# A macaron block on one Trainium2 core: four more turned experts, and a planner with new margins

## The chip, the cores and the metric

The program runs on one core of one Trainium2 chip. A core has TensorE (PE, matrix products into the eight banks of PSUM), VectorE (DVE), ScalarE (ACT), GpSimd (POOL) and SyncE (SP), which issues transfers. Each engine takes its own instructions in order and waits at semaphores for the others. The metric is the time of one execution in microseconds.

## The reference

The block works on 4 sequences of 1024 rows with 128 features in fp32:

```
x = x + 0.5 * ffn(layernorm(x))        # first mixture of experts
x = x + mamba(layernorm(x))            # selective state space layer
x = x + 0.5 * ffn(layernorm(x))        # second one, the same weights

ffn:   cw = softmax(x @ w_router) * softmax(x @ w_gating / 0.1), normalised   # 8 weights per row
       out = sum over e of cw[:, e] * ((silu(x @ w_gate[e]) * (x @ w_up[e])) @ w_down[e])
mamba: h_t = exp(dt_t * A) * h_{t-1} + dt_t * B_t * u_t;  y_t = C_t . h_t     # 256 channels, 16 states
```

All eight experts are computed for every row: F = 512 hidden columns, 128 features.

## The kernel before

**Tiles and positions.** The rows are cut into 8 tiles of 512. Each tile goes once through the first mixture, kind 0, once through the state space layer, and once through the second mixture, kind 1. The 16 passes through a mixture are the positions of ORDER: position 0 is (0, 0), tile 0 first mixture; position 15 is (1, 7).

**Slots.** A position has 32 slots, one for each of 8 experts times 4 chunks of 128 hidden columns; slots are counted through, so position 14 is slots 448 to 479 and position 15 is 480 to 511. In a slot PE makes the gate product (step `first_g`, three products of 512 columns, L839, L840, L842, with high and low parts of the operands), the up product (step `first`, the same three lines) and the down product (step `down`). ACT makes silu of the gate (L1306), DVE multiplies it with up to h (HB, L1113). The gate runs two slots ahead (AHEAD), the down product two slots behind (LAG): in PE's order stand first_g(i+2), first(i), down(i-2).

**Ordinary and turned experts.** In an ordinary expert the down product has h as its stationary operand and is made in fp32, four products of 128 columns (L920); the result lies with rows on partitions. In a turned expert (TURNS) the weights are stationary, the result is transposed, and the down product is three products of 512 columns: high weights with high h (L910), low weights with high h (L912), high weights with low h (L914). For this h is rounded into HI (step `h_hi`) and the remainder made as HL by DVE (`h_lo`, L1069), and the weights of two chunks at a time are split into WDS (`wd_hi`, a rounding, and `wd_lo`, L1081 on DVE). Before the change ACT makes all roundings. WDS has two buffers, HI three.

**Weighing.** The result of an expert is multiplied by its column of weights (step `acc`: L1331 on ACT, L1106 on DVE, L1050 for turned ones) into YE, and added to the tile XT by a transfer that GpSimd issues (L1439). For turned experts the weights must be rows: CW is transposed by PE (`cw_t`, L930), stored to CWD in DRAM and loaded broadcast into YE (`cw_load`, L811); the sum goes into AT, is turned back by four transposes (`t_tr`, L940) and added to XT (`t_add`).

**State space steps.** Each tile has 16 scans (one for each state) of two halves on DVE (`s_b` L1200, `s_scan` L1211, `s_hc` L1219), which need rows of B and C broadcast into BCB by SyncE (`bc_load`, L799, three buffers), and whose results GpSimd's transfers add into Y. `s_yz` closes a tile on DVE (L1231, L1233; for the last tile two additions stand before the product), `s_out` is the output product on PE (L969). The products before the scans are `b_in`, `b_x` and `b_dt`; `b_conv` is the convolution on DVE (L1164). The router of a position is `p_logits` on PE, then `p_max` (L1015 to L1021), `p_exp` on ACT, and `p_norm`, `p_sum`, `p_cw` (L1026 to L1040) on DVE.

**What sets the order.** `timetable()` plays the kernel once with estimated costs, keeping a clock for each engine (`clock`), and writes one list of steps. Each engine's program is that list with the steps that are its own. So a number in the planner moves instructions, and a wait on the chip holds up all that stands behind it on that engine. The planner does not wait for `h_lo` or `wd_lo` when it places `down`. `x_load` brings a later tile into the buffer (XR = 5) of an earlier one and waits in SyncE's queue until the store of that one has landed.

## Time and profile before

| | us |
|---|---|
| median of 3 runs | 1252.88 (1252.73 to 1253.44) |
| the profiled execution | 1252.7 |
| span of its profile | 1250.9 |
| PE busy | 1244.1 (99%) |
| DVE busy | 1131.1 (90%) |
| ACT busy | 1017.1 (81%) |
| POOL busy | 388.4 (31%) |

The span is the time from the first to the last instruction of the program; the execution is 1.8 us longer. PE is on the chain that ended last for 96% of the span. Rows of PE and DVE overlap each other on the same engine, since these engines are pipelined, so the cost of an instruction among others is read from start to start. The granted clock of TensorE is 1.00 in the whole profile, its upper level of 2.4 GHz.

### The profile page before, as it was taken

How to read it: one execution, taken by the hardware profiler on the slowest of the kernel's cores; microseconds unless marked ns; L12 is line 12 of the kernel's file. 1: busy time of each engine (PE TensorE's matmuls, PEld its weight loads, DVE VectorE, ACT ScalarE, POOL GpSimd, SP SyncE). 2: the span in 40 equal slices, each digit the busy share in tenths (PEclk: the TensorE clock that was granted, in tenths of full speed). 3: DMA queues.
4: the chain of work that ended last, by engine and by line, in shares of the span. 5: the costliest groups of instructions: out<-in, count | busy, mean ns of one | idle time of the engine just before them, and what ended most of it. 6: DMA issues, size and time to landing. Idle time of an engine off the chain costs nothing.

```text
span 1250.9 us, 20830 instructions
## 1 busy us (share of the span) xinstructions
PE 1244.1 (99%) x7311; PEld 1076.0 (86%) x7311; DVE 1131.1 (90%) x1524; ACT 1017.1 (81%) x2079; POOL 388.4 (31%) x455
## 2 busy tenths in 40 slices
PE   9999999999999999999999999999999999999998
PEld 6887888888888888888888888888888888888887
DVE  5857699999999999999999999999999989998476
ACT  6777988888987887989978899798987979765664
POOL 0010134234333333334234333352434433332100
PEclk9999999999999999999999999999999999999999
DMA  7412368797878787878898798987979887895132
GB/s 225 105 24 42 87 132 172 144 196 161 168 143 178 161 174 151 177 153 172 164 201 160 153 194 172 186 172 151 199 148 190 154 160 158 161 191 112 28 75 51
DMA packets 116809, 185.90 MB, mean 149 GB/s; under 512 B 11264, under 2 KB 31840, under 8 KB 116704
## 3 DMA queue, kind: packets, MB, share of 16 engines
q0 software_dynamic: 55760, 101.74, 46.1%
q1 hardware_dynamic: 60944, 82.83, 26.4%
q8 instruction: 57, 0.93, 0.3%
q14 instruction: 48, 0.39, 0.1%
HBM read 80.15 MB, written 2.67 MB: 66 GB/s over the span
## 4 chain that ended last, share of the span: by engine, by line
PE 96%; ACT 2%; DVE 1%; issue 1%; DMA 0%; POOL 0%; DVEq 0%; ACTq 0%
PE PS L920 32%; PE PS L839 19%; PE PS L842 19%; PE PS L840 19%; PE PS L969 1%; PE PS L954 1%; PE PS L912 1%; PE PS L914 1%; PE PS L910 1%; PE PS L861 1%; PE PS L871 1%; ACT DA L1401 0%; PE PS L961 0%; ACT HB L1306 0%; DVE HL L1069 0%
## 5 line engine op out<-in xcount | busy, mean ns | idle before, releaser
L920 PEld LDWEIGHTS PS<-WD,HB 128*128 128x128 f32 x3616 | 472.2, 191 | 37.6 <-issue 0.5
L920 PE MATMUL PS<-WD,HB 128*128 128x128 f32 x3616 | 476.0, 274 | 0.0
L1113 DVE TENSOR_TENSOR HB<-PS,HB 128x512 f32<-128x512 f32 x512 | 348.3, 681 | 85.7 <-PE PS L842 72.8
L1306 ACT ACTIVATE HB<-PS 128x512 f32<-128x512 f32 x512 | 294.6, 597 | 111.2 <-PE PS L842 108.7
L1456 POOL DMA_DIRECT2D Y<-HS x252 | 222.1, 958 | 369.2 <-DVE HS L1219 186.4
L839 PE MATMUL PS<-XH,WG 128*128 128x512 f32 x512 | 238.7, 466 | 0.8 <-DVE WG L1120 0.6
L1439 POOL DMA_DIRECT2D XT<-YE x111 | 105.4, 949 | 318.9 <-ACT YE L1331 166.8
L839 PE MATMUL PS<-XH,WU 128*128 128x512 f32 x512 | 203.7, 398 | 0.0
L842 PE MATMUL PS<-XH,WG 128*128 128x512 f32 x512 | 202.2, 395 | 0.0
L842 PE MATMUL PS<-XH,WU 128*128 128x512 f32 x512 | 201.6, 394 | 0.0
L840 PE MATMUL PS<-XH,WG 128*128 128x512 f32 x512 | 200.3, 391 | 0.0
L840 PE MATMUL PS<-XH,WU 128*128 128x512 f32 x512 | 200.3, 391 | 0.0
L1401 ACT ACTIVATE DA<-XS,aneg 128x512 f32<-128x512 f32 x256 | 164.3, 713 | 0.8
L1211 DVE TENSOR_TENSOR_SCAN HS<-DA,car,HS 128x512 f32<-128x512 f32 x128 | 161.8, 1275 | 0.0
L1219 DVE TENSOR_TENSOR HS<-BCB,HS 128x1024 f32<-128x1024 f32 x128 | 156.1, 1220 | 1.4
L1200 DVE TENSOR_TENSOR HS<-BCB,DX 128x1026 f32<-128x1026 f32 (+1 forms) x128 | 155.5, 1220 | 0.2
L1211 DVE TENSOR_TENSOR_SCAN HS<-DA,HS 128x513 f32<-128x513 f32 x128 | 153.8, 1217 | 0.1
L840 PEld LDWEIGHTS PS<-XH,WU 128*128 128x128 f32 x512 | 96.5, 188 | 22.6 <-issue 0.5
L842 PEld LDWEIGHTS PS<-XH,WU 128*128 128x128 f32 x512 | 96.0, 187 | 22.8
L839 PEld LDWEIGHTS PS<-XH,WU 128*128 128x128 f32 x512 | 96.1, 188 | 22.7 <-issue 0.5
L842 PEld LDWEIGHTS PS<-XH,WG 128*128 128x128 f32 x512 | 96.1, 188 | 22.6 <-DVE XH L1171 0.4
L1306 ACT ACT_TABLE_LOAD x87 | 111.6, 1283 | 2.1 <-PE PS L842 0.6
(133 smaller groups left out, 1343.7 us busy)
## 6 DMA issues: line engine op xcount, KB each, us to landing
BCB<-BCD SPq DMA_DIRECT2D x128, 512.0 KB, 5.3
Y<-HS POOLq DMA_DIRECT2D x252, 256.0 KB, 6.3
XT<-YE POOLq DMA_DIRECT2D x111, 256.0 KB, 4.9
YE<-CWD SPq DMA_DIRECT2D x15, 256.0 KB, 4.7
XS<-DX POOLq DMA_DIRECT2D x7, 512.0 KB, 9.0
AT<-YE POOLq DMA_DIRECT2D x11, 256.0 KB, 3.3
XT<-in_L_attn_x_dram SPq DMA_DIRECT2D x8, 256.0 KB, 6.6
WD<-in_L_ffn_w_down_dram SPq DMA_DIRECT2D x8, 256.0 KB, 6.4
```

Source lines behind the costliest of these rows:

```text
L839: pe.matmul(o, w[0], m[0], start=True, stop=False)
L840: pe.matmul(o, w[1], m[0], start=False, stop=False)
L842: pe.matmul(o, w[0], m[1], start=False, stop=True).then_inc(S[sem], 1)
L920: z = pe.matmul(part(g, j), HB[:, i % NH, j * P:(j + 1) * P], WD[:, e, c, :], start=c == 0 and j in firsts, stop=c == FC - 1 and j in lasts)
L1113: v.tensor_tensor(H, up(i), H, ALU.mult).then_inc(S["v_h"], 1)
L1200: v.tensor_tensor(HS[:, m % HR, :, 0:w], rows.unsqueeze(1).broadcast_to([P, 2, w]), DX[:, t % 2, :, 0:w], ALU.mult).then_inc(S["v_db"], 1)
L1211: v.tensor_tensor_scan(H, DA[:, m % NA, j, 0:w], H, car[:, j, n:n + 1] if t % 2 else 0.0, ALU.mult, ALU.add).then_inc(S["v_sc"], 1)
L1219: v.tensor_tensor(H, BCB[:, m % BR, 1, :].unsqueeze(1).broadcast_to([P, 2, T]), H, ALU.mult).then_inc(S["v_hc"], 1)
L1306: a.activation(HB[:, i % NH, :], gate(i), ACT.Silu).then_inc(S["a_sil"], 1)
L1401: z = a.activation(DA[:, m % NA, j, 0:T], XS[:, t % 2, j, 3:3 + T], ACT.Exp, scale=aneg[:, j, n:n + 1])
L1439: gp.dma_start(to, buffer(g), accum_op=ALU.add).then_inc(S["c_acc"], 16)
L1456: gp.dma_start(Y[:, t % 2, j, :], HS[:, m % HR, j, 0:T], accum_op=ALU.add).then_inc(S[f"c_y{j}"], 16)
```

## The change

Experts 4 to 7 of position 14 become turned, so that turned slots run from 464 through 507. Which engine rounds h and the weights is no longer a matter of the position: the planner gives a rounding to ACT where ACT's clock is early, else to DVE. The weights of a pair are split one slot sooner (SPLIT = 2 instead of 1). Turned results other than a run's last are weighed two or three down products later. The passes (1, 3) and (0, 7) change places. The load of a later x tile may be issued from slot 2 of the position before, as soon as the planner has placed the store of the tile whose buffer it takes. Margins of the planner change with it.

```diff
-ORDER = [(0, 0), (0, 1), (0, 2), (0, 3), (1, 0), (0, 4), (1, 1), (0, 5), (1, 2), (0, 6), (1, 3), (0, 7), (1, 4), (1, 5), (1, 6), (1, 7)]
+ORDER = [(0, 0), (0, 1), (0, 2), (0, 3), (1, 0), (0, 4), (1, 1), (0, 5), (1, 2), (0, 6), (0, 7), (1, 3), (1, 4), (1, 5), (1, 6), (1, 7)]
...
-CALM = 0.9
-LATEST = 0.2
+CALM = 0.8
+LATEST = 0.3
...
-TURNS = {0: range(2, 6), 1: range(1, 5), 15: range(0, 7)}
-SCALAR_PARTS = (0, 1, 15)
+TURNS = {0: range(2, 6), 1: range(1, 5), 14: range(4, 8), 15: range(0, 7)}
+EASY = 0.4
+SPLIT = 2
...
+TURN_LATER = 2
+WEIGHED_LATER = {g: BEGIN_LATER if g in TURN_BEGINS else TURN_LATER for g in TURNED if g not in TURN_ENDS}
...
+        if what[0] == "x":
+            yield from until(loaded_x.get(what[1], 0.0))
...
-            at = step("b_add", t, after=at, p=.9) + 7.0
+            at = step("b_add", t, after=at, p=.9) + SUMMED
...
-        scanned[t] = y_at[1]
+        scanned[t] = y_at[1] + SETTLED
...
-        if "scans" in streams and (haste or turn[0] % (3 if passed[0] < NS // 2 else 1) == 0):
+        if HURRY and "scans" not in streams and not begun["scans"]:
+            advance("before")
+        elif "scans" in streams and (haste or turn[0] % (3 if passed[0] < NS // 2 else 1) == 0):
...
     def high(i):
-        on = {"a": .53} if i // SLOTS in SCALAR_PARTS else {"v": .35}
-        hi_at[i] = step("h_hi", i, after=h_at[i], **on)
+        if clock["a"] < h_at[i] + EASY:
+            scalar_rounds.add(i)
+            hi_at[i] = step("h_hi", i, after=h_at[i], a=.53)
+            low(i - 1)
+        else:
+            low(i - 1)
+            hi_at[i] = step("h_hi", i, after=h_at[i], v=.35)
...
+    def split(i):
+        if clock["a"] < clock["pe"] + EASY:
+            scalar_splits.add(i)
+            at = step("wd_hi", i, a=.31)
+        else:
+            at = step("wd_hi", i, v=.2)
+        return at
...
-            if nd % FC == BEGIN_LATER and nd // FC - 1 in TURN_BEGINS:
+            if nd // FC - 1 in WEIGHED_LATER and nd % FC == WEIGHED_LATER[nd // FC - 1]:
...
                 weigh(nd // FC - 1)
-            if (nd + 1) % PAIR == 0 and nd + 1 in TURNED_SLOTS:
...
+            m = nd + SPLIT
+            if m % PAIR == 0 and m in TURNED_SLOTS:
+                split_at[m] = split(m)
+                if m not in scalar_splits:
+                    step("wd_lo", m, v=.4)
...
-        if r == LOADR and p + 1 < NPOS and ORDER[p + 1][0] == 0 and ORDER[p + 1][1] >= XR:
-            step("x_load", ORDER[p + 1][1])
+        if r >= LOADR and p + 1 < NPOS and ORDER[p + 1][0] == 0:
+            t = ORDER[p + 1][1]
+            if t >= XR and t not in asked_x and t - XR in stored_out:
+                asked_x.add(t)
+                loaded_x[t] = max(clock["pe"], stored_out[t - XR] + STORED) + LOADED
+                step("x_load", t)
```

Counted in the built programs, 36 roundings of weights stand on DVE instead of none and 2 on ACT instead of 30; of h, 7 on DVE and 69 on ACT instead of 60 on ACT. There are 76 turned slots instead of 60.

The lines of the changed kernel are numbered 37 higher behind the planner: L1113 is L1150 there, L1069 L1106, L1081 L1118, L1231 L1268, L1233 L1270, L1015 L1052, L1026 L1063, L1040 L1077, L799 L836, L823 L860, L816 L853.

DVE at the closing of the last tile (the first turned slot of position 14, 464; Y<-Y,HS and Y<-Y,SZ are the closing, HB<-PS,HB the product h of a slot, HL and WDS the low parts of h and of the weights). Before:

```order
L1219 TENSOR_TENSOR HS<-BCB,HS 128x2x512
L1113 TENSOR_TENSOR HB<-PS,HB 128x512
L1231 TENSOR_TENSOR Y<-Y,HS 128x1024 x2
L1233 TENSOR_TENSOR Y<-Y,SZ 128x1024
L1113 TENSOR_TENSOR HB<-PS,HB 128x512 x3
```

and now:

```order
L1256 TENSOR_TENSOR HS<-BCB,HS 128x2x512
L1150 TENSOR_TENSOR HB<-PS,HB 128x512 x2
L1268 TENSOR_TENSOR Y<-Y,HS 128x1024 x2
L1270 TENSOR_TENSOR Y<-Y,SZ 128x1024
L1118 TENSOR_TENSOR WDS<-WD,WDS 128x256
L1150 TENSOR_TENSOR HB<-PS,HB 128x512
L1106 TENSOR_TENSOR HL<-HB,HI 128x512
```

The second of the two HB<-PS,HB is h of slot 464; its low part, the last row, stands behind the closing.

DVE at the second half of position 15's router (lg to CW are its softmax and weights), which stands at the end of position 14, slots 478 to 480. Before:

```order
L1113 TENSOR_TENSOR HB<-PS,HB 128x512
L1026 TENSOR_TENSOR lg<-lg 128x4x8
L1028 TENSOR_REDUCE zz<-lg 128x12
L1031 SCALAR_TENSOR_TENSOR sm<-zz 128x4
L1034 TENSOR_TENSOR sm<-sm,zz 128x4
L1038 RECIPROCAL sm<-sm 128x4
L1040 SCALAR_TENSOR_TENSOR CW<-lg,sm 128x32
L1113 TENSOR_TENSOR HB<-PS,HB 128x512 x3
```

and now:

```order
L1102 CAST HI<-HB 128x512
L1063 TENSOR_TENSOR lg<-lg 128x4x8
L1065 TENSOR_REDUCE zz<-lg 128x12
L1068 SCALAR_TENSOR_TENSOR sm<-zz 128x4
L1071 TENSOR_TENSOR sm<-sm,zz 128x4
L1075 RECIPROCAL sm<-sm 128x4
L1077 SCALAR_TENSOR_TENSOR CW<-lg,sm 128x32
L1087 TENSOR_TENSOR YE<-PS,YE 128x512
L1113 CAST WDS<-WD 128x256
L1118 TENSOR_TENSOR WDS<-WD,WDS 128x256
L1150 TENSOR_TENSOR HB<-PS,HB 128x512
L1106 TENSOR_TENSOR HL<-HB,HI 128x512
```

The router's chain has a weighing, a split of weights and two roundings of h for neighbours, and HL of slot 479 is the last row.

SyncE around the store of tile 2 (out_dram) and the load of x tile 7 (XT<-in). Before:

```order
L823 DMA out_dram<-XT 128x4x128
L799 DMA BCB<-BCD 128x2x512 x8
L816 DMA XT<-in_L_attn_x_dram 128x4x128
L799 DMA BCB<-BCD 128x2x512 x9
L792 DMA BCD<-XN 32x512
```

and now:

```order
L836 DMA BCB<-BCD 128x2x512 x11
L860 DMA out_dram<-XT 128x4x128
L853 DMA XT<-in_L_attn_x_dram 128x4x128
L829 DMA BCD<-XN 32x512
L836 DMA BCB<-BCD 128x2x512 x17
```

The load stood eight BCB loads behind the store, and now stands directly behind it.

## Rows read from the trace of the kernel before

**Rows 1.** Windows: span, busy us (x instructions) PE PEld DVE ACT POOL, PEclk, DMA, GB/s.

```profile
160.00:1160.00 1000.00, 999.30 (x6083) 875.76 (x6082) 962.77 (x1205) 841.42 (x1701) 363.49 (x419) 1.00 0.83 166
1141.00:1181.00 40.00, 40.00 (x251) 35.40 (x250) 23.94 (x37) 21.78 (x59) 4.93 (x7) 1.00 0.22 38
```

**Rows 2.** Timeline of PE, ordinary slot: start us, us, engine line op.

```profile
281.76 0.48 PE L839 MATMUL PS<-XH,WG 128*128 128x512 f32 x1
282.08 0.40 PE L840 MATMUL PS<-XH,WG 128*128 128x512 f32 x1
...
284.05 0.48 PE L839 MATMUL PS<-XH,WG 128*128 128x512 f32 x1
```

**Rows 3.** Timeline of PE, a turned slot of position 15.

```profile
1207.28 0.39 PE L839 MATMUL PS<-XH,WG 128*128 128x512 f32 x1
...
1209.34 0.39 PE L839 MATMUL PS<-XH,WG 128*128 128x512 f32 x1
```

**Rows 4.** Timeline of PE, transposes at 1183 and 1244 us.

```profile
1183.40 0.27 PE L930 MATMUL PS<-CON,CW 128*32 128x128 f32 x1
...
1244.46 0.60 PE L940 MATMUL PS<-CON,AT 128*128 128x128 f32 x4
1244.89 2.29 PE L920 MATMUL PS<-WD,HB 128*128 128x128 f32 x19
```

**Rows 5.** Timeline of PE, position 1: waits for WDS, first, third and last.

```profile
102.24 0.50 PE L912 MATMUL PS<-HI,WDS 128*128 128x512 f32 x1
...
117.55 0.39 PE L910 MATMUL PS<-HI,WDS 128*128 128x512 f32 x1
118.20 0.50 PE L912 MATMUL PS<-HI,WDS 128*128 128x512 f32 x1 [0.27 <-DVE WDS L1081]
118.55 0.39 PE L914 MATMUL PS<-HL,WDS 128*128 128x512 f32 x1
...
128.78 0.50 PE L912 MATMUL PS<-HI,WDS 128*128 128x512 f32 x1 [0.32 <-DVE WDS L1081]
```

**Rows 6.** Timeline of DVE among turned slots of position 1.

```profile
117.72 0.42 DVE L1081 TENSOR_TENSOR WDS<-WD,WDS 128x256 fp32r<-128x256 f32 x1
118.06 0.69 DVE L1050 TENSOR_TENSOR YE<-PS,YE 128x512 f32<-128x512 f32 x1
118.66 0.69 DVE L1113 TENSOR_TENSOR HB<-PS,HB 128x512 f32<-128x512 f32 x1
```

**Rows 7.** Timeline of DVE, the product h behind PE at 1183 us.

```profile
1183.67 0.69 DVE L1113 TENSOR_TENSOR HB<-PS,HB 128x512 f32<-128x512 f32 x1 [1.59 <-PE PS L842]
```

**Rows 8.** Groups by line and shape: xcount | busy us, mean ns | idle.

```profile
L1133 DVE CAST WI<-DA 128x512 fp32r<-128x512 f32 x1 | 0.4, 422 | 0.0
...
L1164 DVE SCALAR_TENSOR_TENSOR Y<-XS,cw_t,Y 128x512 f32<-128x512 f32 x48 | 34.6, 745 | 0.0
```

**Rows 9.** Timeline of DVE, the closing of the last tile.

```profile
1149.67 2.55 DVE L1231 TENSOR_TENSOR Y<-Y,HS 128x1024 f32<-128x1024 f32 x2
...
1153.40 1.28 DVE L1113 TENSOR_TENSOR HB<-PS,HB 128x512 f32<-128x512 f32 x2
```

**Rows 10.** Timeline of DVE, router of position 15.

```profile
1173.34 0.31 DVE L1015 STREAM_TRANSPOSE LT<-LR 128x128 f32<-128x128 f32 x1 [0.83 <-ACT LR L1294]
...
1174.55 0.69 DVE L1113 TENSOR_TENSOR HB<-PS,HB 128x512 f32<-128x512 f32 x1
...
1177.43 0.18 DVE L1026 TENSOR_TENSOR lg<-lg 128x32 f32<-128x32 f32 x1
...
1178.55 0.19 DVE L1040 SCALAR_TENSOR_TENSOR CW<-lg,sm 128x32 f32<-128x32 f32 x1
```

**Rows 11.** SyncE: the stores' landing (L823), then its queue's timeline.

```profile
DMA to landing us min/median/max: 2.3/5.7/10.5
...
731.62 0.47 SPq L823 DMA_DIRECT2D out_dram<-XT  x1
737.14 7.20 SPq L799 DMA_DIRECT2D BCB<-BCD  x2
```

More of the change, by code:

```diff
@@ L441, in timetable, with low @@
     nd = 0
-    hi_at = {}
+    hi_at, split_at = {}, {}
     def high(i):
-        on = {"a": .53} if i // SLOTS in SCALAR_PARTS else {"v": .35}
-        hi_at[i] = step("h_hi", i, after=h_at[i], **on)
+        if clock["a"] < h_at[i] + EASY:
[5 more added lines that the diff above has]
+            hi_at[i] = step("h_hi", i, after=h_at[i], v=.35)
+    def low(i):
+        if i in hi_at:
+            step("h_lo", i, after=hi_at[i], v=.6)
+    def split(i):
[5 more added lines that the diff above has]
+        return at
     for i in range(total):
@@ L456, in timetable @@
         h_at[i] = clock["v"] + SIGNAL["v"]
-        if i in TURNED_SLOTS and p in SCALAR_PARTS:
+        if i in TURNED_SLOTS:
             high(i)
-        if i - 1 in hi_at:
-            step("h_lo", i - 1, after=hi_at[i - 1], v=.6)
-        if i in TURNED_SLOTS and p not in SCALAR_PARTS:
-            high(i)
+        else:
+            low(i - 1)
         side()
@@ L466, in timetable @@
             nd += 1
-            if nd % FC == BEGIN_LATER and nd // FC - 1 in TURN_BEGINS:
+            if nd // FC - 1 in WEIGHED_LATER and nd % FC == WEIGHED_LATER[nd // FC - 1]:
+                if nd % SLOTS // FC == 1:
+                    finish("prep")
                 weigh(nd // FC - 1)
-            if (nd + 1) % PAIR == 0 and nd + 1 in TURNED_SLOTS:
-                on = {"a": .31} if (nd + 1) // SLOTS in SCALAR_PARTS else {"v": .2}
-                step("wd_hi", nd + 1, **on)
-                if "v" in on:
-                    step("wd_lo", nd + 1, v=.4)
-            if nd % PAIR == 0 and nd in TURNED_SLOTS and nd // SLOTS in SCALAR_PARTS:
-                step("wd_lo", nd, v=.33)
+            m = nd + SPLIT
[3 more added lines that the diff above has]
+                    step("wd_lo", m, v=.4)
+            m -= 1
+            if m in scalar_splits:
+                step("wd_lo", m, after=split_at[m], v=.35)
             row_loads()
@@ L479, in timetable @@
             elif nd % FC == 0:
-                if nd % SLOTS == FC:
+                if nd % SLOTS == FC and nd // FC - 1 not in TURNED:
                     finish("prep")
-                if nd // FC - 1 not in TURN_BEGINS:
+                if nd // FC - 1 not in WEIGHED_LATER:
                     weigh(nd // FC - 1)
@@ L494, in timetable @@
                 step("small_load")
-            if r % 2 and 25 <= r <= 29:
-                step("set", (r - 25) // 2, v=1.4)
-        if r == LOADR and p + 1 < NPOS and ORDER[p + 1][0] == 0 and ORDER[p + 1][1] >= XR:
-            step("x_load", ORDER[p + 1][1])
+        if i in SETS:
+            step("set", SETS.index(i), v=1.4)
+        if r >= LOADR and p + 1 < NPOS and ORDER[p + 1][0] == 0:
[4 more added lines that the diff above has]
+                step("x_load", t)
         if p + 1 < NPOS and r >= (PREP if p != 1 else LATER) and p + 1 not in prepared:
@@ L514, in timetable @@
     run(tail(NPOS - 1))
-    return steps, scalar_weighs
+    return steps, scalar_weighs, scalar_rounds, scalar_splits
 class Waits:
@@ L533, in macaron_program @@
     of = out.rearrange("b (t j p) d -> (b t) p j d", t=2, j=SUB)
-    steps, scalar_weighs = timetable()
+    steps, scalar_weighs, scalar_rounds, scalar_splits = timetable()
     with ExitStack() as ctx:
@@ L663, in rows_loads @@
             return f"c_cw{BUFFERED.index(g) % 2}", 16 * len(same)
-        def scalar_part(i):
-            return i // SLOTS in SCALAR_PARTS
         def wait_high(eng, i):
-            sem = "a_hh" if scalar_part(i) else "v_hh"
-            eng.wait_ge(S[sem], sum(k <= i and scalar_part(k) == scalar_part(i) for k in TURNED_SLOTS))
+            by_scalar = i in scalar_rounds
+            same = [k for k in TURNED_SLOTS if k <= i and (k in scalar_rounds) == by_scalar]
+            eng.wait_ge(S["a_hh" if by_scalar else "v_hh"], len(same))
         def wait_weights_high(eng, i):
-            sem = "a_wd" if scalar_part(i) else "v_wh"
-            eng.wait_ge(S[sem], sum(k <= i and scalar_part(k) == scalar_part(i) for k in TURNED_SLOTS if k % PAIR == 0))
+            by_scalar = i in scalar_splits
+            same = [k for k in TURNED_SLOTS if k <= i and k % PAIR == 0 and (k in scalar_splits) == by_scalar]
+            eng.wait_ge(S["a_wd" if by_scalar else "v_wh"], len(same))
         def pair(i):
@@ L1060, in _ @@
                     v.tensor_tensor(X, X, bank(b), ALU.add).then_inc(S["v_at"], 1)
-                elif k == "h_hi" and not scalar_part(s[1]):
+                elif k == "h_hi" and s[1] not in scalar_rounds:
                     i = s[1]
@@ L1070, in _ @@
                                     ).then_inc(S["v_hl"], 1)
-                elif k == "wd_hi" and not scalar_part(s[1]):
+                elif k == "wd_hi" and s[1] not in scalar_splits:
                     i = s[1]
@@ L1312, in _ @@
                     a.activation(LR[0:SUB * E, :], bank(b)[0:SUB * E, 0:P], ACT.Copy).then_inc(S["a_ct"], 1)
-                elif k == "h_hi" and scalar_part(s[1]):
+                elif k == "h_hi" and s[1] in scalar_rounds:
                     i = s[1]
@@ L1317, in _ @@
                     a.activation(HI[:, TURNED_SLOTS[i] % HI_RING, :], HB[:, i % NH, :], ACT.Copy).then_inc(S["a_hh"], 1)
[L1318 removed]
+                elif k == "wd_hi" and s[1] in scalar_splits:
                     i = s[1]
```

19 lines of the change are left out of this document (14 added, 5 removed).

## The prediction

> **What bounds the kernel now.** I read the windows first. In the thousand microseconds in which the state space stages run, TensorE (PE) is busy 999.3 us and VectorE (DVE) 962.8 us [rows 1], so the time is PE's list of products plus whatever PE waits, and the waits are small. What has to be counted is products removed, products added, and waits lost or gained. In the stretch where the four experts are turned (about 1141 to 1181 us) DVE was busy 23.9 us of 40 [rows 1], which looks like ample room for the new work. A mean over 40 us says nothing about single places, though, and DVE takes its instructions strictly in order, so I then followed DVE's order through the new slots, with the timeline of DVE and PE for the spacing.
>
> **The change part by part.**
>
> *Removed: one product per turned slot.* An ordinary slot is six products of 512 columns and four fp32 ones that the trace shows as eight. From one L839 to the same point a slot later it takes 284.05 - 281.76 = 2.29 us, in which L839 to L840 is 0.32 us instead of the 0.23 us that such a product needs elsewhere, a loss of 0.09 us behind fp32 products [rows 2]. A turned slot is nine products of 512 columns: 1209.34 - 1207.28 = 2.06 us [rows 3], with no such loss. Saved per slot 0.23 us; 16 slots: -3.7 us, all on PE, which is the bound.
>
> *Added on PE.* Position 14 gets its own transposes: four of AT, 1244.89 - 1244.46 = 0.43 us, plus 0.09 us for the product behind them, since they now stand among 512 column products; and one of the weights, which at 0.43/4 comes to 0.11 us [rows 4]. The output product of the last tile (s_out, fp32) now also stands among 512 column products: 0.09 us. Together +0.7 us. Net on PE: -3.0 us.
>
> *Waits that go: weights split a slot sooner.* In position 1, PE waits in four slots between L910 and L912 for the low part of the weights (WDS from L1081). The first ends at 102.24, the last at 128.78; in the third L910 to L912 takes 118.20 - 117.55 = 0.65 us where an undisturbed step is 0.23, and the product behind it is late as well, 0.35 instead of 0.23 us [rows 5]. Read in the same way the four exceed the undisturbed step by 0.25, 0.11, 0.42 and 0.49 us, and with some 0.1 us each behind them that is 1.7 us. With the split issued one slot sooner DVE has a slot (2.06 us) more than it needs, so all four go: -1.7 us. What is late next is the low part of h (HL, read by L914).
>
> *Waits that come.* For each new or changed place I add up DVE's instructions from the product h of a slot to its own HL, and compare with what PE does from the end of that slot's up product to L914. Prices are start to start, since a row's duration overlaps the next: a full width operation 118.66 - 118.06 = 0.60 us, the low split of a weight pair 118.06 - 117.72 = 0.34 us [rows 6]. h starts 0.27 us after PE's next product, L930 at 1183.40 against 1183.67 [rows 4, 7], and 0.05 us more pass before PE starts: WDS ends at 117.72 + 0.42 = 118.14, L912 starts at 118.20 [rows 5, 6]. A cast of 512 columns lasts 0.42 us, taken as 0.35 start to start, one of 256 as 0.20 [rows 8].
>
> Place A, slot 464, the first turned one. The closing of the last tile (two adds, one product) stands between h(464) and the split. It costs 1153.40 - 1149.67 = 3.73 us [rows 9], since each waits for the one before. DVE: h 0.60 + 3.73 + WDS 0.34 + h(465) 0.60 + HL 0.68 to its end + 0.32 = 6.27 us. PE gets there after two ordinary slots and two products: 4.58 + 0.46 = 5.04 us. PE waits 1.2 us, with the late product behind it 1.3 us. Before, no turned slot was here, and the closing cost PE nothing.
>
> Place B, slots 477 to 479. The router of position 15 now stands among turned slots. DVE: four h 2.40, three HL 1.80, the last to its end 0.68, the maximum chain 1174.55 - 1173.34 = 1.21, the softmax chain L1026 to L1040 1178.55 - 1177.43 and the start of the next, 1.23 [rows 10], two weight pairs 1.08, two casts of h on DVE 0.70, one weighing 0.60, latency 0.32: 10.02 us. PE: four turned slots and two products, 8.24 + 0.46 = 8.70 us. PE waits 1.3 us, 1.4 with the product behind.
>
> Place C, slots 44 to 47, position 1: five h 3.00, four HL 2.40 and 0.68, six convolution steps at 0.66 (0.75 us each [rows 8], less the same 0.09 of overlap), a copy 0.07, two weighings 1.20, two weight pairs 1.08, latency 0.32: 12.71 us. PE: five turned slots, six products of b_in and two more, 10.30 + 1.38 + 0.46 = 12.14 us. 0.6 us, with what is late behind 0.7 us.
>
> These three cost +3.4 us. They are bounds from below where DVE comes late to the place, from above where PE has been held up for other reasons between; both unknowns I put at 0.5 us each way.
>
> Here a rule of the Trainium skill is weighed, VectorE: DVE Perf Modes, section The DRAIN you can't avoid: an instruction does not start until the pipe of the one before has emptied. The row shows 0.60 us from start to start of instructions of 0.69 us [rows 6], so here the next one starts before the row's end, and the measurement decides. What it would make of the time stands with the rivals.
>
> *Edits costed at nothing.* Rounding by timetable moves 28 weight casts from ScalarE to DVE and some castings of h; their DVE time is in A, B and C, and elsewhere in the turned stretches a pair of slots has 4.11 us for at most 4 h or HL (2.40) + 0.54 + a weighing 0.60 = 3.54 us. If that cover were gone, each pair would cost the difference. Weighing two products later: the expert's bank is read again a slot group later (8.2 us), so 4.1 us more are free; only B's weighing lies on a bad place, and it is counted. The new AT and YE transfers go through GpSimd's and SyncE's queues after the last scan transfer, where nothing of DVE waits for them. The swap of (1,3) and (0,7) and the new margins of the planner re-order the middle. There PE was idle 0.7 us of 1000 [rows 1]; overlapping rows hide short waits, so the gain is at most some 2 us, and a loss as large is as likely. I take 0.
>
> *The x tile.* In the new order the load of tile 7 stands directly behind the store of tile 2 in SyncE's queue and waits until that store has landed; behind it stand a row store (BCD) and the loads of BCB that DVE needs. The next such load followed the store by 737.14 - 731.62 = 5.5 us before, and stores land in 2.3 to 10.5 us, median 5.7 [rows 11]. At the median plus two issues of 0.4 us the BCB load is 1.0 us late, and I take that as hidden by the three buffers of BCB; at 10.5 us it is 5.8 us late. Bounds 0 and +5.8 us; I take 0, the row of the median being nearest.
>
> **Sum.** -3.7 + 0.7 - 1.7 + 3.4 = -1.3 us. On the profiled execution, 1252.7 us with a span of 1250.9 us, that is 1251.4 us; on the median of the runs, 1252.88 us, it is **1251.6 us**. A measurement of this kernel can tell about 0.2%, 2.5 us, from no change, so my forecast lies within it.
>
> **Rivals.**
>
> *The waits A and B do not appear* (the planner's order gives DVE enough lead, or PE is late there for other reasons). Then -3.7 + 0.7 - 1.7 + 0.7 = -4.0 us: 1248.9 us. For it: DVE was busy 60% in that stretch [rows 1]. Against it: h cannot start before its product, so DVE's lead does not help; the sums start there. With only one of the two: 1250.3 us. Chance 0.21 in all.
>
> *The store holds SyncE's queue.* The load of x waits for the store at 10.5 us, BCB is 5.8 us late, and DVE, 96% busy there [rows 1], stands still with the products h behind that row's first operation; PE's product two slots on waits for h. It decides from a store landing of about 6 us. At worst -1.3 + 5.8 = +4.5 us, 1257.4 us; at 8 us 3.3 us late: 1254.9 us. This is the case on the slower side. For it: stores that long exist. Against it: the buffers. Chance 0.12, of which 0.07 over 2.5 us slower.
>
> *DVE's instructions do not overlap in the new mixture.* Each then costs its whole row: 0.69 us for h, HL and a weighing, 0.42 for WDS and a wide cast, 0.75 for a convolution step [rows 6 to 8]. A comes to 1.5 us, B to 2.4, C to 2.5, with the products behind 6.7 instead of 3.4 us: +2.0 us, 1254.9 us. Against it: the very instructions of the turned slots stand 0.60 us apart [rows 6]. Chance 0.03. This is what the page named above would give.
>
> *The split is not sooner in effect.* If the casts wait for the bank (each waits for the product that frees its buffer), PE still waits at L912: the 1.7 us stay, 1253.3 us. Chance 0.08. The Trainium skill, SBUF — State Buffer, section Who interferes with whom, says that an fp32 copy from SBUF to SBUF on DVE holds GpSimd off, descriptors included, and that the second to come waits wholly. By that rule each of the 43 new casts could hold a transfer's issue for its own length, or be held by it. No row of this case shows it.
>
> **How the numbers follow.** Forecast, between 1250.4 and 1253.2 us: 0.56. Waits absent 0.21, queue 0.12, splits 0.08, no overlap 0.03. The range takes in one of A and B missing together with a gain in the middle (1249.4) and the queue's case at 8 us (1254.9): 1249.4 to 1254.9. Faster by over 0.2% (under 1250.4): the first rival, 0.21, with 0.01 from the middle. Slower by over 0.2%: 0.07 of the queue. Within: 0.71.
>
> **What the new profile would show.** Right: sixteen more slots of 2.06 us; PE waiting about 1.2 us for HL, between the second and the third product of a turned slot, around 1148 us and again around 1181 us, with no wait for WDS in position 1 but one for HL; SyncE's load of x issued 5 to 8 us behind the store. Wrong: turned slots of position 14 without a wait (the sums' start is wrong), waits for WDS again (buffers, not order), or DVE waiting for BCB near 740 us. A new PE wait of more than 2 us in the middle would break the zero that I took there.

## The result, and the profile after

The changed kernel takes 1256.13 us (median of 10 runs, 1254.23 to 1257.52), the kernel before in the same session 1252.91 us (10 runs, 1252.20 to 1254.15): a ratio of 1.0026, 95% interval 1.0017 to 1.0034. It is slower by about 3.2 us, and the forecast of 1251.6 us, with its range of 1249.4 to 1254.9 us, was wrong. The profiled execution took 1255.67 us with a span of 1253.9 us, against 1252.7 and 1250.9 us.

All line numbers are 37 higher than before. The windows answer to [rows 1]; the third shows where the time went. Columns: span, busy us (x instructions) of PE, PEld, DVE, ACT, POOL, PEclk, DMA share, GB/s.

```profile
160.00:1160.00 1000.00, 998.75 (x6061) 874.54 (x6060) 969.60 (x1221) 843.42 (x1693) 368.74 (x417) 1.00 0.81 166
...
1141.00:1181.00 40.00, 39.07 (x189) 31.63 (x189) 34.79 (x66) 25.28 (x59) 3.72 (x5) 1.00 0.19 42
...
130.00:160.00 30.00, 28.11 (x163) 24.14 (x162) 21.28 (x31) 27.57 (x60) 5.16 (x8) 1.00 0.35 91
```

The middle is as busy as before. Where position 14's experts are turned, DVE went from 23.9 to 34.8 us of 40 and PE stood still for 0.9 us. Between 130 and 160 us, a stretch that the prediction did not look at, PE stood still for 1.9 us. The waits of PE name it (line, releaser, us in total, times, longest):

```profile
PE PS L951 <- DVE HL L1106: 2.0, 3, 1.1
PE PS L977 <- DMA AT<-YE: 1.9, 1, 1.9
...
PE PS L977 <- DVE AT L1092: 1.2, 1, 1.2
```

The first line holds the waits that were forecast. The other two, 3.1 us, were not: L977 are the transposes with which a group of turned experts ends, in position 1 and at the end of the kernel. None of the rows of before shows PE waiting there.

I also went through all products of both traces, 7311 before and 7236 after, from start to start, and took from each the median step of its kind in the kernel before, as the undisturbed one (0.23 us for 512 columns, 0.32 behind fp32, 0.11 for fp32 of 128 columns). The undisturbed steps come to 1238.1 us before and 1235.4 us after, so the product saving is there, 2.7 us. What lies above them went from 7.9 to 13.6 us. The prices below called an excess are from this reckoning; an excess is that of the wait alone, and the product behind a wait for HL or WDS is late by another 0.10 to 0.11 us each time.

**The forecast waits.** PE at places A, B and C, and a turned slot (answering [rows 3]):

```profile
1147.43 0.40 PE L947 MATMUL PS<-HI,WDS 128*128 128x512 f32 x1
1147.94 0.50 PE L949 MATMUL PS<-HI,WDS 128*128 128x512 f32 x1
1149.14 0.50 PE L951 MATMUL PS<-HL,WDS 128*128 128x512 f32 x1 [0.70 <-DVE HL L1106]
...
1183.14 0.39 PE L949 MATMUL PS<-HI,WDS 128*128 128x512 f32 x1
1184.67 0.50 PE L951 MATMUL PS<-HL,WDS 128*128 128x512 f32 x1 [1.14 <-DVE HL L1106]
...
118.00 0.50 PE L951 MATMUL PS<-HL,WDS 128*128 128x512 f32 x1
...
120.53 0.50 PE L951 MATMUL PS<-HL,WDS 128*128 128x512 f32 x1 [0.18 <-DVE HL L1106]
...
1207.03 0.39 PE L876 MATMUL PS<-XH,WU 128*128 128x512 f32 x1
...
1209.11 0.39 PE L876 MATMUL PS<-XH,WU 128*128 128x512 f32 x1
```

Excess at A 0.28 + 0.97 = 1.25 us, at B 1.30 us, at C 0.13 + 0.34 = 0.47 us. The forecast counted the products behind as well; with them it is A 1.35 us (forecast 1.3), B 1.41 us (1.4) and C 0.86 us (0.7), where a third, shorter wait follows at 124.8 us. A turned slot takes 2.08 us (2.06). DVE at place A, where the closing stands ahead of the low part of the weights and of h:

```profile
1143.14 0.69 DVE L1150 TENSOR_TENSOR HB<-PS,HB 128x512 f32<-128x512 f32 x1 [0.82 <-PE PS L879]
1143.74 2.55 DVE L1268 TENSOR_TENSOR Y<-Y,HS 128x1024 f32<-128x1024 f32 x2
1146.33 1.23 DVE L1270 TENSOR_TENSOR Y<-Y,SZ 128x1024 f32<-128x1024 f32 x1
1147.47 0.42 DVE L1118 TENSOR_TENSOR WDS<-WD,WDS 128x256 fp32r<-128x256 f32 x1
1147.81 0.68 DVE L1150 TENSOR_TENSOR HB<-PS,HB 128x512 f32<-128x512 f32 x1
1148.41 0.68 DVE L1106 TENSOR_TENSOR HL<-HB,HI 128x512 fp32r<-128x512 f32 x1
```

HL ends at 1149.09, and PE's L951 starts at 1149.14. The step from h to HL is 0.60 us, as in [rows 6].

**The waits nobody forecast.** AT collects what the turned experts of a position produce, by transfers that add YE into it, issued by GpSimd (POOL) one after the other: each waits until the one before has landed. These are the three of position 1, before and then after (start us, us from issue, what POOL waited for):

```profile
119.05 0.86 POOL L1439 DMA_DIRECT2D AT<-YE  x1 [20.45 <-DVE YE L1050]
129.62 0.85 POOL L1439 DMA_DIRECT2D AT<-YE  x1 [9.71 <-DVE YE L1050]
138.49 0.86 POOL L1439 DMA_DIRECT2D AT<-YE  x1 [8.02 <-DMA AT<-YE]
```

```profile
123.24 0.86 POOL L1476 DMA_DIRECT2D AT<-YE  x1 [24.05 <-DVE YE L1087]
132.84 0.85 POOL L1476 DMA_DIRECT2D AT<-YE  x1 [8.74 <-DVE YE L1087]
141.69 0.86 POOL L1476 DMA_DIRECT2D AT<-YE  x1 [7.99 <-DMA AT<-YE]
```

The second one lands 8.3 us after its issue in both, the third 3.25 us after. In both kernels the third waits for the second, so the end of the chain moves with the weighing of expert 3, which DVE now does at 131.86 instead of 128.64 us. The third lands at 138.49 + 3.25 = 141.74 us before, at 141.69 + 3.25 = 144.94 us after. PE's transposes, first before the change and then after it:

```profile
143.34 0.60 PE L940 MATMUL PS<-CON,AT 128*128 128x128 f32 x4
```


```profile
142.12 1.05 PE L957 MATMUL PS<-WD,HB 128*128 128x128 f32 x8
145.07 0.63 PE L977 MATMUL PS<-CON,AT 128*128 128x128 f32 x4 [1.89 <-DMA AT<-YE]
```

An excess of 2.06 us. Before, AT was there 1.6 us ahead of PE; it now comes 3.2 us later, and PE is ready for it 0.3 us earlier. At the end of the kernel the last transfer into AT has DVE as its next link (POOL, then DVE, then PE); the transfer before it had landed at 1236.4 us and holds nothing up:

```profile
1242.25 0.86 POOL L1476 DMA_DIRECT2D AT<-YE  x1 [8.34 <-issue]
```

```profile
1240.39 0.68 DVE L1087 TENSOR_TENSOR YE<-PS,YE 128x512 f32<-128x512 f32 x1
...
1246.60 0.69 DVE L1092 TENSOR_TENSOR AT<-AT,YE 128x512 f32<-128x512 f32 x1 [1.94 <-DMA AT<-YE]
```

```profile
1247.44 0.63 PE L977 MATMUL PS<-CON,AT 128*128 128x128 f32 x4 [1.22 <-DVE AT L1092]
```

Before, that weighing stood at 1235.11 and its transfer at 1236.09 us. Excess 1.39 us. Three things add up here: the weighing is two products later, the transfer is issued 1.86 us behind the start of its weighing instead of 0.98, and it lands 4.26 us after its issue instead of 3.30. The first is the edit; what the other two come from, no run shows.

**The clock behind the wait.** In 7 of the 10 runs the mean granted clock of TensorE was 0.999 (1255.98 to 1257.52 us), in the other three 1.0 (1254.23, 1255.17, 1255.67 us), medians 1256.41 and 1255.17 us; in the kernel before it was 1.0 in all. The profiled execution of after shows nothing of it; that of e7, which has the same wait, does (PE, then the window and, below it, the same stretch of the changed kernel's own profile):

```profile
144.81 0.63 PE L977 MATMUL PS<-CON,AT 128*128 128x128 f32 x4 [1.94 <-DMA AT<-YE]
145.19 0.61 PE L876 MATMUL PS<-XH,WG 128*128 128x512 f32 x1
145.61 0.63 PE L877 MATMUL PS<-XH,WG 128*128 128x512 f32 x1
146.03 0.63 PE L879 MATMUL PS<-XH,WG 128*128 128x512 f32 x1
```

```profile
144.80:148.20 3.40, 3.39 (x13) 2.81 (x14) 2.69 (x3) 2.42 (x5) 0.00 (x0) 0.59 0.02 5
```

```profile
144.80:148.20 3.40, 3.13 (x20) 2.85 (x21) 2.43 (x3) 2.99 (x6) 0.00 (x0) 1.00 0.02 5
```

Behind the wait the granted clock is at its lower level, 1.2 instead of 2.4 GHz (0.59 on the mean of this window), and a step takes 0.42 us instead of 0.23. Six such steps are 1.2 us.

### The profile page after: what moved, and what is told of

Its sections match the earlier page's. It is cut to its first block, busy times and chain, and to the rows that moved or that the text cites. A ratio compares the mean times of both kernels' runs of the same rounds, so it can differ in the third digit from the quotient of the medians.

```text
span 1253.9 us, 20727 instructions
## 1 busy us (share of the span) xinstructions
PE 1242.1 (99%) x7236; PEld 1071.0 (85%) x7236; DVE 1159.2 (92%) x1598; ACT 1011.0 (81%) x2037; POOL 395.0 (32%) x454
## 4 chain that ended last, share of the span: by engine, by line
PE 92%; DVE 2%; DMA 2%; ACT 2%; issue 1%; SPq 0%; DVEq 0%; POOLq 0%; ACTq 0%
PE PS L957 30%; PE PS L876 18%; PE PS L879 18%; PE PS L877 18%; DMA AT<-YE 2%; PE PS L1006 1%; PE PS L951 1%; PE PS L991 1%; PE PS L947 1%; PE PS L949 1%; PE PS L898 1%; PE PS L908 1%; DVE HB L1150 1%; DVE HL L1106 1%; ACT L1343 0%
## 5 line engine op out<-in xcount | busy, mean ns | idle before, releaser
L957 PEld LDWEIGHTS PS<-WD,HB 128*128 128x128 f32 x3488 | 455.7, 191 | 36.6 <-issue 0.5
L957 PE MATMUL PS<-WD,HB 128*128 128x128 f32 x3488 | 459.2, 274 | 0.0
L1150 DVE TENSOR_TENSOR HB<-PS,HB 128x512 f32<-128x512 f32 x512 | 347.8, 680 | 62.8 <-PE PS L879 46.8
```

Source lines behind the costliest of these rows:

```text
L957: z = pe.matmul(part(g, j), HB[:, i % NH, j * P:(j + 1) * P], WD[:, e, c, :], start=c == 0 and j in firsts, stop=c == FC - 1 and j in lasts)
L1150: v.tensor_tensor(H, up(i), H, ALU.mult).then_inc(S["v_h"], 1)
```

## The experiments

Theory: the loss is the late weighing, by the chain of transfers into AT, at two places, with the lower clock behind the first; the product saving and the waits A, B and C are as forecast. Rivals: the turned experts of position 14 cost more than they save; the splits or the new order do. Every time below is a median of 11 runs unless said otherwise, beside the kernel before in the same session: 1252.74 us for e1 to e4, 1252.76 for e5 to e8, 1253.11 for e9 to e12.

### The late weighing taken back, in whole and by place

e1: every weighing at once, but for the first expert of a group, which was late before the change too.

```diff
-WEIGHED_LATER = {g: ... for g in TURNED if g not in TURN_ENDS}
+WEIGHED_LATER = {g: ... for g in TURN_BEGINS}
```

> The changed kernel with the turned results weighed as before the change: right after the last down product of their expert, the first of a run one product earlier; the rest of the change stays. Theory (the later weighing makes the two turns back late: PE waits 2.06 us for the transfer into AT before position 1's transposes, 1.39 us for the last sum at the end, and the weighing lies in the router's place at slot 479): both waits go, and the wait at slot 479 shrinks from 1.3 to about 0.7 us, so 4.0 us less than the changed kernel, about 1252.1 us, and the transfers into AT are issued 3 to 4 us earlier. Rival (the casts on DVE hold GpSimd off, or its queue is late for another reason): the waits for AT stay above 1 us each and the time stays above 1254.5 us.

Measured 1252.77 us, ratio 1.0000 (0.9990 to 1.0009). Both waits for AT are gone and the clock is 1.0 in all runs. The casts are all still on DVE, so the rival, that they hold GpSimd off, is out as the cause of these waits. Two things moved beside them: B fell from 1.30 to 0.28 us, since the late weighing had also stood behind the router's chain on DVE, and C grew from 0.47 to 1.44 us:

```profile
122.11 0.50 PE L951 MATMUL PS<-HL,WDS 128*128 128x512 f32 x1 [0.77 <-DVE HL L1106]
```

So the late weighing was the whole loss, 3.4 us, and it had a use: it kept DVE free ahead of C. The planner also wrote parts of positions 0 and 1 in another order here (52 to 131 us); e9 and e11 below come without that.

e6: at once in positions 0 and 1 only. e7: at once in positions 14 and 15 only.

```diff
-... for g in TURNED if g not in TURN_ENDS}
+... for g in TURNED if g not in TURN_ENDS and (g in TURN_BEGINS or g // E > 1)}    # e6
+... for g in TURNED if g not in TURN_ENDS and (g in TURN_BEGINS or g // E < 14)}   # e7
```

> The changed kernel with the weighing at once in positions 0 and 1 only; positions 14 and 15 weigh later, as in the changed kernel (1256.1 us). The theory, that the late transfer of AT in position 1 costs its wait of 2.06 us and the stretch at the lower clock behind it (1.25 us in seven of ten executions, 0.9 on the mean), and that the weighings now at once add 1.4 us of waits for HL at places in positions 0 and 1: 1256.1 - 2.06 - 0.9 + 1.4 = 1254.5 us, the mean granted clock 1.0 in every execution, and the wait of 1.39 us before the last transposes still there. The rival, that the lower clock comes from elsewhere: 1255.4 us with executions below 1.0.

> The changed kernel with the weighing at once in positions 14 and 15 only. The theory: the wait of 1.39 us before the last transposes goes and place B falls from 1.30 to 0.28 us, and nothing else moves: 1256.1 - 1.39 - 1.02 = 1253.7 us, with a wait of 2.06 us at 145 us still there and a mean clock under 1.0 in about two executions of three. The rival, that the wait at the end of the kernel is hidden by something else that ends as late (the last weighing, the last store): 1255.0 us.

Measured: e6 1254.57 us (1.0016, 1.0007 to 1.0025), clock 1.0 in all 11 runs; e7 1253.68 us (1.0009, 1.0000 to 1.0018), clock under 1.0 in 4 of 11 runs. Both are within 0.1 us of the theory's numbers, e7 in part by luck: the clock was to be low in two runs of three, and the median fell into a run without it. One detail missed: in e6 the last wait for AT was 0.38 us in the profile, not 1.39; the transfer landed 3.25 us after its issue instead of 4.26, and that is the difference. In e7 the seven runs at clock 1.0 have a median of 1253.15 us, the four others 1255.05 us: 1.9 us apart, where the profile of one such run shows 1.2 us of slow steps.

e9: e1 with one instruction moved, the weighing of expert 3 of position 1, two products later.

```diff
-... for g in TURN_BEGINS}
+... for g in TURNED if g in TURN_BEGINS or g == 11}
```

> e1 (every weighing at once, 1252.8 us) with one single instruction moved: the weighing of expert 3 of position 1, the next to the last of its turned ones, two products later. On VectorE it changes place with the four instructions h, HL, h, HL; nothing else in the program moves. The theory, that this one weighing sets the wait for AT before the transposes of position 1: the wait of about 2.06 us comes back at 145 us, and with it the lower clock in part of the executions, 0.6 to 0.9 us on the median: 1252.8 + 2.06 + 0.7 = 1255.6 us. The rival, that a transfer started 3 us later is hidden or that the whole chain of late weighings is needed: 1253.3 us or less.

Measured 1254.44 us, ratio 1.0010 (1.0001 to 1.0019) where e1 has 1.0000. The orders of PE, ACT and POOL in the trace are those of e1, and that of DVE differs in the one instruction. The wait is back, from this one instruction, but it is 1.17 us, not 2.06, and the clock stays at 1.0 in all runs:

```profile
134.88 0.85 POOL L1476 DMA_DIRECT2D AT<-YE  x1 [12.20 <-DVE YE L1087]
142.83 0.86 POOL L1476 DMA_DIRECT2D AT<-YE  x1 [7.10 <-DMA AT<-YE]
```

The theory had the place right and the size wrong. The second transfer landed 7.4 us after its issue instead of 8.3, and that is the 0.9 us. The lower clock was never seen behind this shorter wait.

e8 was to find the best mixture: only the next to the last weighing of each group at once.

```diff
+... and (g in TURN_BEGINS or g + 1 not in TURN_ENDS)}
```

> The changed kernel with the weighing at once for one expert of each turned position, the next to the last; all others later, as in the changed kernel. The theory, that of the chain of transfers into AT only the weighing before the last but one counts, says that both waits for AT go and that places B and C stay as in the changed kernel: 1256.1 - 2.06 - 0.9 - 1.39 = 1251.8 us. The rival, that every link of the chain is late, since each waits for the landing of the one before: the waits for AT shrink by less than half and the time is about 1254.5 us.

Measured 1265.34 us (4 runs), ratio 1.0100. The waits for AT are gone, as the theory says, but the planner wrote another order from position 1 on, in the middle too, and the closing of the last tile came late:

```profile
1170.68 3.75 PE L1006 MATMUL PS<-WO,Y 128*128 128x128 f32 x16 [4.57 <-DVE Y L1270]
1184.03 0.63 PE L898 MATMUL PS<-CON,XN 128*128 128x128 f32 x4 [2.58 <-ACT XN L1313]
```

As a trial of the idea it says nothing; the order had to be held fixed.

### The turned experts of position 14

e2: the changed kernel without them. e5: the same, with every weighing at once.

```diff
-TURNS = {0: range(2, 6), 1: range(1, 5), 14: range(4, 8), 15: range(0, 7)}
+TURNS = {0: range(2, 6), 1: range(1, 5), 15: range(0, 7)}
```

> The changed kernel without the four turned experts of position 14; all other parts stay. Theory (turning them saves 3.0 us net on PE and costs waits of 1.25 us at slot 464 and 1.3 us at slot 479, so it is worth only some -0.4 us): the time rises by 0.4 us to about 1256.5 us, both waits are gone, the wait of 2.06 us before position 1's transposes and that of 1.39 us at the end stay. Rival (the turned experts of position 14 are themselves what costs): the time falls below 1255 us.

> The changed kernel with every weighing at once (as in e1, 1252.8 us) and without the four turned experts of position 14. My costing of the turned experts of position 14: 16 slots -3.7 us, transposes and mode change +0.7, place A +1.25 and what was left of place B in e1, +0.3: they are worth -1.5 us, so this kernel takes 1254.3 us. The rival, drawn from e2 against the changed kernel, is that the turned experts of position 14 cost about a microsecond more than they save: then it takes 1251.6 us. If it stands at 1254.3, e2's loss was the lower clock's, which some executions show and others don't, and not the experts'.

Measured: e2 1254.94 us (1.0018, 1.0009 to 1.0027), e5 1253.86 us (1.0009, 1.0000 to 1.0018). e2 came out where the rival had it, below 1255 us; e5 stands by the theory. With late weighing the experts cost 1.2 us (1256.13 against 1254.94), without it they save 1.1 us (1252.77 against 1253.86). The first number mixes two clocks, since the lower one fell in 7 of 10 runs of the changed kernel and in 5 of 11 of e2: of the runs at 1.0 alone the medians are 1255.17 and 1254.48 us, of the others 1256.41 and 1255.64, so that the experts cost 0.7 to 0.8 us. The traces show the terms. The experts save 2.7 us of undisturbed steps. Against that stand A 1.25 and, weighed late, B 1.30, a wait of 0.28 us at 1172.76 and the 1.39 us for AT at the end, which e2 does not have: +1.5 us, more than the medians show. Weighed at once it is A 1.25 and B 0.28 and 0.10: -1.1 us. My expectation for e2 let the 1.39 us stay, and so was wrong by about as much. Position 15 weighs late in e2 as well; but there the last transfer was issued 1.00 us behind its weighing's start and landed in 3.30 us, and DVE and PE hardly waited. So the late weighing alone does not make the wait at the end. With the later issue added it is 0.38 us (e6), and only with the slower landing as well 1.39 us.

e10: e1 with three turned experts in position 14, beginning behind the closing.

```diff
-14: range(4, 8)
+14: range(5, 8)
```

> e1 with three turned experts in position 14 instead of four (5 to 7), so that the closing of the last tile no longer stands between turned slots. The theory: place A, 1.25 us, goes; four slots lose their 0.23 us each, +0.92: 1252.8 - 0.33 = 1252.5 us, with no wait for WDS or HL near 1148 us. The rival, that the closing makes PE late wherever the turned slots begin, since DVE needs 3.73 us for it: a wait of about 1.2 us behind 1150 us, and 1253.7 us.

Measured 1254.45 us, ratio 1.0010 (1.0001 to 1.0019): a miss. Place A is gone as told, but the group's first weighing now stands between the halves of the router's chain on DVE (1173.75 us) and a second one behind it (1177.77 us), both ahead of the HL that PE waits for, and B is 1.83 us instead of 0.28, with 0.46 us for AT at 1193 us:

```profile
1179.70 0.50 PE L951 MATMUL PS<-HL,WDS 128*128 128x512 f32 x1 [1.67 <-DVE HL L1106]
```

e3 put the turned experts of position 14 into the kernel before, with nothing else.

```diff
-TURNS = {0: range(2, 6), 1: range(1, 5), 15: range(0, 7)}
-SCALAR_PARTS = (0, 1, 15)
+TURNS = {0: range(2, 6), 1: range(1, 5), 14: range(4, 8), 15: range(0, 7)}
+SCALAR_PARTS = (0, 1, 14, 15)
```

> The kernel before with experts 4 to 7 of position 14 turned and nothing else of the change; all roundings there on ScalarE. Theory: net -3.0 us on PE, and one wait of about 2.3 us where the last tile's closing (3.73 us of DVE) now stands between two turned slots, none at the router (DVE 4.0 us against 4.6 us of PE); the four waits for WDS in position 1 stay. So -0.7 us, 1252.2 us. Rival (the closing is hidden by DVE's lead): -3.0 us, 1249.9 us.

Measured 1266.93 us (4 runs), ratio 1.0113. Neither theory foresaw it:

```profile
1163.63 0.50 PE L912 MATMUL PS<-HI,WDS 128*128 128x512 f32 x1 [3.20 <-DVE WDS L1081]
1185.47 1.09 PE L861 MATMUL PS<-CON,XN 128*128 128x128 f32 x4 [7.36 <-ACT XN L1276]
```

The planner of before puts the closing ahead of a split of the weights and the norm of position 15 late on ScalarE, and the lower clock follows twice (mean 0.83 from 1155 to 1195 us). In the changed kernel no wait of such a length is there. So the other edits, those costed at nothing among them, are what lets the four experts stand in position 14 at this price; which of them does it, no run separates.

### The split alone

e4: the kernel before with the split of the weights a slot sooner.

```diff
-            if (nd + 1) % PAIR == 0 and nd + 1 in TURNED_SLOTS:
-                on = {"a": .31} if (nd + 1) // SLOTS in SCALAR_PARTS else {"v": .2}
-                step("wd_hi", nd + 1, **on)
...
+            if (nd + 2) % PAIR == 0 and nd + 2 in TURNED_SLOTS:
+                step("wd_hi", nd + 2, a=.31)
+            if (nd + 1) % PAIR == 0 and nd + 1 in TURNED_SLOTS:
+                step("wd_lo", nd + 1, v=.33)
```

> The kernel before with the weights split one slot sooner, both halves on the same engines as before, and nothing else of the change. Theory: the four waits between the first and the second product of turned slots in position 1 go, 1.7 us with what follows them: 1251.2 us. Rival (the low part of h is late next at the same places, since the DVE work is the same): PE then waits for HL there and less than 1 us is gained, above 1251.9 us.

Measured 1263.58 us (4 runs), ratio 1.0081 (line numbers 3 lower than before). The waits for WDS are gone, and PE waits for HL instead, with an excess of 0.64 us at 54 us (position 0) and 0.43 us at 125 us (position 1), as the rival had it. The 10 us come from elsewhere: the planner wrote another order, and ScalarE is late with a norm.

```profile
81.29 0.79 PE L836 MATMUL PS<-XH,WG 128*128 128x512 f32 x1 [2.48 <-ACT XH L1281]
81.88 0.63 PE L837 MATMUL PS<-XH,WG 128*128 128x512 f32 x1
```

The lower clock follows here too. The split's own worth is therefore read from the changed kernel's trace and not from this run.

### A kernel that beats both

e11: all late weighings of positions 0 and 1 but that of expert 3 of position 1, and none in 14 and 15. In the traces PE's order is that of the changed kernel up to 1172 us, and DVE's up to 1167 us but for the one weighing.

```diff
-... for g in TURNED if g not in TURN_ENDS}
+... for g in TURNED if g in TURN_BEGINS or g in (3, 4, 10)}
```

> e1 with three weighings later again: experts 3 and 4 of position 0 and expert 2 of position 1; expert 3 of position 1 and all of positions 14 and 15 stay at once. The theory: the waits for HL behind 116 us fall from 1.44 to the 0.47 us of the changed kernel, that at 54 us (0.20) goes, and there is no wait for AT: 1252.8 - 1.2 = 1251.6 us. The rival, that the earlier links of the chain of transfers count as well: a wait for AT of 1 us or more at 145 us, and 1252.8 us or more.

Measured 1251.13 us (1250.66 to 1251.49), ratio 0.9984 (0.9975 to 0.9993), 2.0 us faster than the kernel before and 5 us faster than the changed one. The transfers of position 1 and PE's transposes:

```profile
123.47 0.86 POOL L1476 DMA_DIRECT2D AT<-YE  x1 [24.03 <-DVE YE L1087]
127.79 0.85 POOL L1476 DMA_DIRECT2D AT<-YE  x1 [3.46 <-DVE YE L1087]
137.55 0.85 POOL L1476 DMA_DIRECT2D AT<-YE  x1 [8.91 <-DVE YE L1087]
```

```profile
143.21 0.60 PE L977 MATMUL PS<-CON,AT 128*128 128x128 f32 x4
```

The second one now lands in 3.55 us, and the third waits for its data and no longer for the second. The first link is as late as in the changed kernel (123.47 us) and costs nothing: the rival, that every link counts, is out. B falls here too, to 0.27 us.

e12: e11 with three turned experts in position 14 and every rounding of h on ScalarE.

```diff
-14: range(4, 8)
+14: range(5, 8)
-        if clock["a"] < h_at[i] + EASY:
+        if True:
```

> e11 with three turned experts in position 14 and every rounding of h on ScalarE (eight fewer casts on VectorE, two of them at place C and four at place B). The theory: 1251.6 - 0.33 for place A, - 0.28 for what is left of place B, - 0.3 at place C (a cast of 0.35 us less ahead of HL): 1250.7 us. The rival, that ScalarE is late with h's high part, 0.53 us of work behind h where VectorE needs 0.35, and PE then waits for HI: 1251.6 us or more.

Measured 1252.01 us, ratio 0.9992 (0.9983 to 1.0001), 0.9 us slower than e11. No wait for HI appears, so not the rival's reason: C keeps its 0.47 us, and B is 1.34 us, with two weighings at the router's chain as in e10.

## Why the prediction was wrong

**Product saving: right.** -2.7 us against -3.0; a turned slot is 2.08 us and not 2.06.

**Split a slot sooner: right.** No wait for WDS is left in position 1. The four had an excess of 1.27 us, and each product behind them 0.10 us: 1.7 us, as forecast.

**Places A, B, C: right.** With the products behind 1.35, 1.41 and 0.86 us, in all 3.6 against 3.4, and 0.3 us at 1172.76 us that no term covered. Adding up DVE's instructions from h to HL at start-to-start prices was good to 0.2 us. The rival without A and B is out, and that of DVE's instructions without overlap as well: the steps are 0.60 us. By the rule of the Trainium skill, VectorE: DVE Perf Modes, section The DRAIN you can't avoid, A would have been 1.5 us and B 2.4; the traces do not agree.

**"Weighing two products later": the step that failed.** It stood among the edits costed at nothing, with a cover of 8.2 us, the time until the expert's bank is read again. That names the wrong consumer. The weighing has a second one: its YE goes by transfer into AT, each transfer waits for the one before to land, and PE transposes AT at the group's end. What the cover was could be read in the trace of before: the third transfer was issued only when the second had landed (8.02 us of waiting for it), and landed at 141.74 us, 1.6 us before PE's transposes at 143.34. At the end of the kernel the last transfer landed at 1236.09 + 3.3 = 1239.4 us and was read at 1243.12, a cover of 3.7 us:

```profile
1243.12 0.69 DVE L1055 TENSOR_TENSOR AT<-AT,YE 128x512 f32<-128x512 f32 x1
```
After the change the transfer is issued at 1242.25 us, 6.2 us later, of which 1.6 us is the lag of the whole kernel there (PE's product ahead of the transposes starts at 1245.82 instead of 1244.23), 3.7 us the later weighing and 0.9 us a later issue behind it, and it lands 4.3 us behind its issue instead of 3.3: 5.6 us later in all, 1.9 more than the cover. That is DVE's wait of 1.94 us. Cost: 2.06 + 1.39 us, of which the first comes with the late weighing alone and the second needs the later issue and the slower landing as well, 1.9 us together. The next sentence said that nothing of DVE waits for the new transfers. It left out the old ones, which the same edit makes late: L1092 waits 1.94 us for the last one of position 15.

**The lower clock behind a wait: not foreseen.** No rival held it. The runs with it and those without have medians 1.2 us apart in the changed kernel, 1.2 in e2 and 1.9 in e7.

**The order and margins: right as to size, wrong as to why.** From 200 to 1100 us the excess of steps over 0.06 us fell from 4.5 to 3.4 us, and the many smaller ones rose by 0.8 us in the whole trace, 0.6 of it by the turned slots of position 15: nearly nothing in sum. But in e3, e4 and e8 the order that the planner then wrote cost 9 to 14 us. That the middle stayed within 2 us because these margins had been set for this very set of edits is my reading; no run shows it.

**The x tile: right in its 0 us, the lateness behind it too small.** SyncE's queue, answering [rows 11], and DVE behind it:

```profile
728.45 0.47 SPq L860 DMA_DIRECT2D out_dram<-XT  x1
733.92 0.37 SPq L853 DMA_DIRECT2D XT<-in_L_attn_x_dram  x1
736.76 0.32 SPq L829 DMA_DIRECT2D BCD<-XN  x1
737.12 0.43 SPq L836 DMA_DIRECT2D BCB<-BCD  x1
```

```profile
743.46 1.23 DVE L1237 TENSOR_TENSOR HS<-BCB,DX 128x1026 f32<-128x1026 f32 x1 [0.31 <-DMA BCB<-BCD]
```

The load follows the store by 5.47 us. The next load of BCB follows it by 8.67 us, 3.15 us later than before and not 1.0, since the row store (BCD) ahead of it is issued only at 736.76 us. DVE then waits 0.31 us for BCB, a sign that the prediction had named for the rival, and PE does not wait. So the buffers hid almost all of a lateness that the rival, with a store of 8 us, counts in full. What a store of 10 us would do, this execution does not show.

**The casts and GpSimd.** The issues of AT<-YE lasted 847/856/927 ns (least, median, most) before and 852/858/929 ns after. By the Trainium skill, SBUF — State Buffer, section Who interferes with whom, the added casts could hold such an issue off; these rows show nothing of it. Nor is a cast beside the issue at 1242.25 us, which is 0.9 us late behind its weighing: the last one on DVE ahead of it ended at 1236.5 us.

**The sum with the measured terms.** -2.7 for the steps, -1.7 WDS, +3.6 places A to C, +0.3, +3.45 for AT, -1.1 in the middle, +0.8 for the small ones, +0.4 in the first 100 us, whose excess differs by as much between kernels alike there (3.1 us in the changed one, 3.3 in e11, 2.8 in e12): +3.05 us, where the spans differ by 3.0. Without the AT term it is -0.4 us, which is 0.9 us above the forecast and inside its range. e11, which undoes the failed step where it costs and keeps the rest, was measured at 1251.13 us, where the prediction had 1251.6; that it comes so near is in part luck, since in e11 B is 1.0 us less than forecast.

What stays open: why a turned slot takes 2.08 us in the changed kernel's position 15 and 2.06 in the kernel before, why the last transfer into AT is issued 0.9 us later behind its weighing and lands 1.0 us slower, and why the granted clock falls in some executions and not in others that have the same wait.

## What to carry to other kernels

Before an instruction is moved later, list every reader of what it writes, transfers included, and follow each chain to the engine that sets the end; in a chain of transfers in which each waits for the landing of the one before, look for the link at which the issuing engine does wait for that landing (8.02 us here, on the second of three), for that link moves all behind it, while the first had time to spare. Compare the time at which the last link lands with the time at which it is read; that difference, and not the nearest reader's, is the cover. Where a planner writes the order, an edit made alone can cost ten microseconds by the order that it sets off, as in e3, e4 and e8: look for the form of the edit that leaves the order elsewhere as it is, and compare only such kernels.

## What the runs showed of the hardware

A wait of PE of 2 us can cost more than itself. After a wait of 2.06 to 2.1 us in position 1 the granted clock fell to its lower level in 7 of 10 runs of the changed kernel, 5 of 11 of e2 and 4 of 11 of e7, and a product of 512 columns then took 0.42 us instead of 0.23; after a wait of 1.17 us (e9) it fell in none of 11. The Trainium skill, TensorE: Matmul & The Clock Gate, Part 1, names the two levels, 1.2 and 2.4 GHz, and gives 426.7 ns from start to start for 512 columns at the lower one. The trace agrees, with its steps of 0.42 to 0.43 us.

The same 256 KB transfer, AT<-YE, landed in 3.2 to 8.3 us after its issue in the changed kernel and in 3.2 to 3.9 us in e11. The slow one is issued at 132.84 us, beside three loads of BCB that SyncE issues from 130.69 us; issued at 127.79 us, ahead of them, it took 3.55 us. In the kernel before, issued at 129.62 us, 1.9 us behind the first of the three loads, it took 8.3 us as well. So an issue ahead of the loads brought the faster transfer. That the loads are the cause is argued from their times alone; no run took them away.
